# Transposed tiles of x read from DRAM, and two tiles centred after their transpose, in the first layer of a graph network

## What is computed

```python
h = relu(layernorm(x))
# layer 0 (relational convolution)
n = ln_weight * (h * rsqrt(mean(h*h) + 1e-6))
y = n @ W_root + bias + sum over r of segment_mean(n[src] @ W_rel[r], dst)   # r = 0, 1; width 286
x = x + h + elu(y) @ wo_weight
# layer 1 (attention)
g = relu(layernorm(x));  p = g @ W_gat
e = exp(-leaky_relu(p@a_l [src] + p@a_r [dst]))
x = x + g + elu(segment_sum(e * p[dst], src) / (segment_sum(e, src) + 1e-5))
```

## Time and profile before

| | us |
|---|---|
| median of 3 runs | 515.64 |
| the runs | 514.94 to 517.17 |
| the profiled execution, its own time | 514.97 |
| its span | 513.2 |
| PE busy | 495.4 (97%) |
| DVE busy | 374.9 (73%) |
| ACT busy | 226.7 (44%) |
| POOL busy | 74.7 (15%) |

### The profile page before, as it was taken

The page is one execution under the profiler, slowest core; times in us unless marked ns, Lnnn a source line. Parts: engine busy times, 40 slices in busy tenths (PEclk is TensorE's granted clock), DMA queues, the critical chain, the costliest instruction groups (busy, mean ns, idle before and its releaser), DMA issues.

```text
span 513.2 us, 7812 instructions
## 1 busy us (share of the span) xinstructions
PE 495.4 (97%) x2983; PEld 426.2 (83%) x2983; DVE 374.9 (73%) x644; ACT 226.7 (44%) x382; POOL 74.7 (15%) x72
## 2 busy tenths in 40 slices
PE   3999999999999999999999999999999999999996
PEld 2889989988989988898788888888887888888886
DVE  4846885598889999997865555556598878777633
ACT  5865443415966666667632222224233333223211
POOL 1362213100000000000000000000083333322400
PEclk9999999999999999999999999999999999999999
DMA  9872273404013235247911111100022222222211
GB/s 259 228 239 81 80 228 117 127 1 114 2 47 112 84 99 143 81 123 277 319 53 40 41 41 41 41 0 0 1 80 82 83 90 69 81 80 81 70 53 44
DMA packets 22186, 49.15 MB, mean 96 GB/s; under 512 B 4798, under 2 KB 10709, under 8 KB 22018
## 3 DMA queue, kind: packets, MB, share of 16 engines
q1 hardware_dynamic: 20879, 44.66, 29.2%
q10 hardware_dynamic: 1008, 3.67, 2.0%
q0 software_dynamic: 256, 0.26, 0.2%
HBM read 33.05 MB, written 16.85 MB: 97 GB/s over the span
## 4 chain that ended last, share of the span: by engine, by line
PE 86%; DVE 7%; DMA 4%; ACT 2%; issue 1%; SPq 0%; ACTq 0%; DVEq 0%
PE ps L1328 11%; PE ps L1593 9%; PE ps L1595 9%; PE ps L1594 9%; PE ps L1487 8%; PE ps L1574 7%; PE ps L1575 7%; PE ps L1576 7%; PE ps L1397 4%; PE ps L1416 2%; DMA x_scratch<-xt 1%; PE ps L1546 1%; DMA xt<-xh_scratch 1%; PE ps L1560 1%; PE ps L1548 1%; PE ps L1547 1%
## 5 line engine op out<-in xcount | busy, mean ns | idle before, releaser
L1593 PE MATMUL ps<-h_hi,att_hi 125*125 125x512 f32 (+1 forms) x190 | 73.5, 387 | 0.0
L1594 PE MATMUL ps<-h_lo,att_hi 125*125 125x512 f32 (+1 forms) x190 | 72.6, 382 | 0.0
L1595 PE MATMUL ps<-h_hi,att_lo 125*125 125x512 f32 (+1 forms) x190 | 72.5, 382 | 0.0
L1574 PE MATMUL ps<-wg,gT_hi 128*125 128x512 f32 x160 | 63.8, 399 | 0.3 <-DVE wg L1097 0.3
L1575 PE MATMUL ps<-wg,gT_hi 128*125 128x512 f32 x160 | 63.1, 394 | 0.0
L1576 PE MATMUL ps<-wg,gT_lo 128*125 128x512 f32 x160 | 63.0, 394 | 0.0
L1487 PE MATMUL ps<-msg_hi,adj_hi 125*125 125x288 f32 x180 | 50.3, 303 | 0.2 <-ACT adj_hi L596 0.2
L1487 PE MATMUL ps<-msg_lo,adj_hi 125*125 125x286 f32 x180 | 45.9, 295 | 0.0
L471 POOL TENSOR_TENSOR some<-first_att 125x625 f32<-125x625 f32 x1 | 2.4, 2440 | 277.8 <-DVE first_att L1157 277.8
L691 ACT ACTIVATE em<-ps,rinv 125x512 f32<-125x512 f32 (+1 forms) x21 | 14.0, 669 | 64.2 <-DVE hp L1201 64.2
L1595 PEld LDWEIGHTS ps<-h_hi,att_lo 125*125 125x125 f32 x190 | 35.2, 186 | 7.9
(11 more groups left out here) (215 smaller groups left out, 1116.6 us busy)
## 6 DMA issues: line engine op xcount, KB each, us to landing
xt<-in_x SPq DMA_DIRECT2D x10, 448.0 KB
xh_scratch<-xt SPq DMA_DIRECT2D x10, 448.0 KB
xt<-xh_scratch SPq DMA_DIRECT2D x10, 448.0 KB
x_scratch<-xt SPq DMA_DIRECT2D x10, 448.0 KB
x1t<-x_scratch SPq DMA_DIRECT2D x10, 448.0 KB
xr<-x_scratch SPq DMA_DIRECT2D x10, 448.0 KB
out_x<-xr SPq DMA_DIRECT2D x19, 224.0 KB
wg_raw<-in_L_gnn_W ACTq DMA_DIRECT2D x7, 512.0 KB, 7.4
```

What stands on the lines that cost most here:

```text
L1574: M.matmul(to, hi, wg[k][:, 0, cut], start=n == 0, stop=False)
L1593: M.matmul(to, hi[:, s, :], h_hi[:, s, cut], start=s == 0, stop=False)
L1594: M.matmul(to, hi[:, s, :], h_lo[:, s, cut], start=False, stop=False)
L1595: return M.matmul(to, lo[:, s, :], h_hi[:, s, cut], start=False, stop=s == TILES - 1)
```

## The change

- The host hands the kernel a second copy of x, `x_turned`, in which each tile is already transposed (128 partitions, 8 parts of 125 columns). For tiles 4 to 9 SP loads it into `x_t` (`load_x_turned`), a DMA of 500 KB per tile.
- For these tiles PE transposes nothing. It spreads the tile's mean over the partitions of a PSUM bank with one matmul (`means`). DVE subtracts it (`centred`), ACT takes the relu into `hT_hi` (`high_parts`), DVE makes `hT_lo` from `x_t` and `hT_hi` (`turned_low_parts`). The layer norm's scale, which is positive, is left out there and multiplied into the second scale by a small operation in `mean_square`.
- Tiles 0 and 1 are treated alike, but PE transposes the raw x as it comes (`raw_transposed`), ACT copies the mean out of PSUM (`spread`), and DVE's `raw_centred` subtracts it in halves. Their `deviation` and `norm`, which now serve only the residual and the second scale, stand behind the split of most of the weights.
- Tiles 2 and 3 stay as they were.
- `picked` and `windows_transposed` move on PE into the middle of the products of tiles 6 and 8, and `total` into `last_products`. On DVE, `first_rows` is cut in another place.
- At the seam, ACT's `load_wg(6)` and `load_wg(7)` stand behind parts of `turned`, and both engines split weight part 4 one call earlier.

```diff
+            def load_x_turned(t, b):
+                sp.wait_ge(S["hT_lo_rdy"], data(t - 2 if t >= TURNED + 2 else b))
+                sp.dma_start(x_t[b][:], x_turned[t].rearrange("p (k n) -> p k n", n=T)).then_inc(S["xt_in"][b], 16)
...
             for t in range(AHEAD, TILES):
                 store_xh(t, t % 2)
                 if t + 2 < TILES:
                     load_x(t + 2, t % 2)
+                if TURNED + 2 <= t + 1 < TILES:
+                    load_x_turned(t + 1, (t + 1) % 2)
...
+            def high_parts(t, b):
+                act.wait_ge(S["centred"], t - TURNED + 1)
+                act.wait_ge(S["g_ps"], room(t))
+                A.activation(hT_hi[b][:], x_t[b][:], ACT.Relu).then_inc(S["hT_hi_rdy"], 1)
...
+            def raw_centred(t, h):
+                dve.wait_ge(S["hT_ps"], data(t))
+                dve.wait_ge(S["spread"], t + 1)
+                V.tensor_tensor(x_t[t][:, 4 * h:4 * h + 4, :], first_tp(t, h), mean_b[t][:].unsqueeze(1).broadcast_to([P, 4, T]),
+                                ALU.subtract).then_inc(S["raw_centred"], 1)
+            def first_low_parts(t, h, came_in, many, signal):
+                dve.wait_ge(S[came_in], many)
+                V.scalar_tensor_tensor(hT_lo[t][:, 4 * h:4 * h + 4, :], x_t[t][:, 4 * h:4 * h + 4, :], 0.0,
+                                       hT_hi[t][:, 4 * h:4 * h + 4, :].bitcast(F32), ALU.max, ALU.subtract).then_inc(S[signal], 1)
             def mean_square(t):
                 dve.wait_ge(S["rm_rdy"], data(t))
-                V.reciprocal(stats1[:, bass.ds(t, 1), 5], stats1[:, bass.ds(t, 1), 5]).then_inc(S["rms_rdy"], 1)
+                last = V.reciprocal(stats1[:, bass.ds(t, 1), 5], stats1[:, bass.ds(t, 1), 5])
+                if not 2 <= t < TURNED:
+                    last.then_inc(S["rs1_rdy"], 1)
+                    dve.wait_ge(S["rs1_rdy"], t + 1 if t < 2 else t - TURNED + 3)
+                    last = V.tensor_tensor(stats1[:, bass.ds(t, 1), 5], stats1[:, bass.ds(t, 1), 5], stats1[:, bass.ds(t, 1), 2], ALU.mult)
+                last.then_inc(S["rms_rdy"], 1)
+            def centred(t, b):
+                dve.wait_ge(S["xt_in"][b], (t - b) * 8 + 16 - 8 * TURNED)
+                dve.wait_ge(S["mean_ps"], t - TURNED + 3)
+                V.tensor_tensor(x_t[b][:], x_t[b][:], bank(b, P, T).unsqueeze(1).broadcast_to([P, KT, T]), ALU.subtract).then_inc(S["centred"], 1)
+            def turned_low_parts(t, b):
+                dve.wait_ge(S["hT_hi_rdy"], data(t))
+                V.scalar_tensor_tensor(hT_lo[b][:], x_t[b][:], 0.0, hT_hi[b][:].bitcast(F32), ALU.max, ALU.subtract).then_inc(S["hT_lo_rdy"], 1)
+            def step1(t):
+                centred(t, t % 2)
+                messages(t - 2, t % 2, t // 2 - 1)
+                turned_low_parts(t, t % 2)
+                mean_square(t)
+                if t + 1 < TILES:
+                    moments(t + 1, 1 - t % 2, (t + 1) // 2)
...
             def stage1(first, end):
-                pipeline((transposed, 1), (products, 2), steps=(first, end))
+                for t in range(first, end):
+                    products(t, t % 2, t // 2)
+                    if t + 2 < TILES:
+                        means(t + 2)
```

More of the change, by code:

```diff
@@ L49, in rgcn_gat_kernel @@
     AHEAD = 4
+    TURNED = 4
     BAND = 112
@@ L151, in rgcn_gat_kernel @@
         zero_adj_of.close()
+        turned_of = ExitStack()
+        sb(turned_of, "below_x_t", [P, XT_AT // 2], BF16)
+        x_t = [sb(turned_of, f"x_t{b}", [P, KT, T], F32) for b in range(2)]
+        turned_of.close()
         counts = sb(ctx, "counts", [T, TILES, N], U16)
@@ L226, in rgcn_gat_kernel @@
             ("some", [T, TILES // 2, T], F32))
+        mean_b = [over("junk", 32 + 512 * b, f"mean_b{b}", [P, T]) for b in range(2)]
         w_raw, wo_raw = over("w_lo", 0, "w_raw", [P, KT, 2, FB]), over("wo_lo", 0, "wo_raw", [FT, 2, D])
@@ L569, in _ @@
             pads()
-            pipeline((transposed, 1), (messages, 2), (normed, -1), steps=(AHEAD, TILES + 1))
+            transposed(3, 1, 1)
+            for t in range(AHEAD, TILES):
+                messages(t - 2, t % 2, t // 2 - 1)
+                high_parts(t, t % 2)
+                if t + 1 < TILES:
+                    normed(t + 1, 1 - t % 2, (t + 1) // 2)
+            messages(TILES - 2, 0, TILES // 2 - 1)
             for g in range(NG):
@@ L1361, in products @@
                 for n in range(2):
+                    if n == 1 and t == 6:
+                        picked()
+                    if n == 1 and t == TILES - 2:
+                        windows_transposed()
                     last = split_products(bank(2 + 2 * b + n, T, FB), [
@@ L1419, in last_products @@
                 pe.wait_ge(S["zero_used"], NG)
-            first_transposed()
-            products_of(0, 0)
-            transposed(1, 1, 0)
-            products_of(0, 1)
-            for k in range(0, 2):
-                products_of(1, k)
-            for k in range(2, 7):
+            for t in range(2):
+                raw_transposed(t)
+                raw_means(t)
+            for t in range(2):
+                for k in range(0, 3):
+                    products_of(t, k)
+            for k in range(3, 7):
                 products_of(0, k)
@@ L1432, in _ @@
             products_of(1, 7)
-            stage1(AHEAD, 8)
-            picked()
-            stage1(8, 10)
-            windows_transposed()
-            stage1(10, 11)
-            total()
+            transposed(3, 1, 1)
+            stage1(2, TILES - 1)
             last_products()
```

143 lines of the change are left out of this document (90 added, 53 removed).

## The result

| kernel | median of 6 runs | lowest to highest | profiled execution | its span | granted clock |
|---|---|---|---|---|---|
| before | 516.04 us | 514.94 to 517.17 | 514.97 us | 513.2 us | 0.998 |
| changed | 525.30 us | 523.26 to 526.12 | 523.56 us | 521.7 us | 0.990 |

The change makes the kernel slower: 1.0164 times as long, 95% interval 1.0143 to 1.0185, that is 8.5 us with 7.4 to 9.5 (the two medians of the table are 9.3 apart). I had forecast 518.4 and a range up to 521.0. The direction was right, the size was not. The two profiled executions are 8.6 apart (8.5 in span), so they are a fair pair to look for the time in.

The account below looks back on a forecast made before the run. PE, busy 97% of the span, was taken to bound the kernel, with its waits. 514.97 + 5.7 (start) - 4.1 (stage 1) + 3.0 (tail) - 1.2 (seam) = 518.4 us; range 513.3 to 521.0.

Parts of the forecast that it names:

- The start: Up to PE's products of tile 2: late norm of tile 2 and DVE held by POOL's residuals, +5.7 us.
- toss-up: Whether residual(0) catches deviation(1)'s two-input operation, 0.04 us behind its earliest start: +5.0 if not, +6.4 if caught; middle taken.
- Stage 1: From tile 2's products to the last tile's: transposes of six tiles removed, mean matmuls added, fewer low-part waits, -4.1 us.
- 0.3 for tile 9's statistics: Within stage 1's sum: PE waits 0.3 us for the statistics of tile 9.
- loads of transposed tiles come late: Rival: tile 8's x_t load stands behind a store queued behind window-span DMAs; 1 to 2 us more on DVE, 520.5; chance 0.15.
- The tail: End of stage 1: PE's window groups wait for DVE's keys and first rows, +2.7, plus total moved there, +0.3.
- The seam: PE's 1.03 wait behind ACT's loads of weight parts 6 and 7 goes: -1.2 us, at worst 0.
- would take it back: At the seam: PE's 0.29 wait for a weight part would cancel the gain, had DVE not moved part 4 ahead.
- One-column operations aren't held: Rival at the start: residuals don't hold one-column DVE operations; tile 2's products at 38.1, sum 516.2; chance 0.17.
- No DVE operation of the start meets a residual: Rival at the start: no holds there, tile 2's products at 36.3, sum 513.5; chance 0.18.
- the signs I had named for being right: Tile 2's product near 40, norm(2) past 32, L946 and L948 over 1 us, 9.7 product spacing, window-group idling, no 1.03 seam wait.
- The signs I had named for being wrong: Products of tile 2 before 37, PE waiting for a low part between tiles 4 and 8, window groups without a wait.

Follow-up runs that it names:

- no_meetings: Changed kernel, with POOL starting its residuals of tiles 0 to 2 each only after the next tile's deviation is made: 1.0066 of before, 520.17 us.
- six_tiles: Changed kernel without its start: tiles 0 and 1 normed and then transposed as in the kernel before: 1.0007 of before, 516.93 us.
- kept_busy: Changed kernel with matmuls nobody reads put into four of PE's waits, the waits themselves kept: 1.0092 of before, 521.59 us.
- pauses: Kernel before, with PE made to wait twice for nothing it needs, behind the products of tiles 3 and 5: 1.0133 of before, 523.36 us.
- early_loads: Changed kernel, each transposed tile's load put ahead of the store of the tile before on SP's queue: 1.0157 of before, 524.90 us.
- loads_residual: early_loads, with POOL starting the residual of tile 8 only behind DVE's low part of tile 8: 1.0123 of before, 522.56 us.
- early_norms: Changed kernel, deviations and norms of tiles 0 and 1 moved ahead of weight part 4 on ACT, part 3 on DVE: 1.0091 of before, 521.29 us.
- six_best: six_tail, with the statistics of tile 9 made ahead of the messages of tile 6 on DVE: 1.0055 of before, 519.56 us.
- all_mended: Changed kernel with early norms, residuals 0 and 1 right behind them, 2 and 3 behind tile 3's deviation, and six_tail's stage 1 end: 1.0020 of before, 517.68 us.
- six_tail: six_tiles with early loads, residual(8) behind low part 8, windows transposed before tile 8's products, keys before tile 7's messages: 0.9979 of before, 514.69 us.

## Why the prediction was right and wrong

**The start, +5.7 forecast, +6.7 measured: the mechanism held.** norm(2) was late because DVE and ACT made the first norms behind weight parts, and DVE was held by POOL. no_meetings, which takes only the holds away, moved the first product by 4.1. The toss-up fell on its upper side: the one-column operation came 0.02 behind the residual's start and was caught. The middle that I took was a value the kernel could not have; of a coin with sides at 5.0 and 6.4 one side has to be named. That is 0.7 of the 1.0. The other 0.3 fit the statistics of tile 1, for which I let DVE go from one tile to the next, while x of tile 1 came 1.04 us later.

**Stage 1, -4.1 forecast, -1.1 measured: the step that failed.** The removed and added work was as priced: without the wait for the mean (2.13) and the half clock behind it (1.70) the stretch gives -4.9, against the -4.4 of my terms without the 0.3 for tile 9's statistics. That 0.3 was 2.13. I had the mechanism as the last rival, "loads of transposed tiles come late", at 0.15, but gave it 1 to 2 us "on DVE, which has them to spare until the keys". I followed DVE's queue forward to the keys and left out that the statistics of tile 9 stand in it, with PE waiting for them long before. On the cause of the late load I was half right. On SP's queue it stood behind another load, which I had not seen, and that one waited for the store of tile 7 to land. But the store did take 7.3 with the spans' copy under way, against 3.1 and 4.0 for the two before it; in the kernel before and in six_tiles the store behind the spans took 7.3 and 7.4 too. That the spans slowed it is argued from this, not tried. The rival had nearly the right event, at 2.1 in its sum, where wait and clock together cost 3.5.

**No term for the clock.** PE's waits were priced at their own length. In the sum a wait of 2 to 3 us can cost 1.7 more. kept_busy shows it in this kernel and pauses in the one before, though in kept_busy's profile 1.0 of the 1.75 won came back as a longer wait for the first window group: this term and the tail's lean on each other. The changed kernel's profiled execution came 5.2 above my sum; one such stretch on PE's path is 1.7 of it, the wait ahead of that stretch 1.8 (2.13 less the 0.3). The profiled execution has the highest granted clock of the changed kernel's six, 0.990 against a median of 0.9865. That is 1.8 us of full clock more in the median, an estimate, and the median time is 1.7 above the profile. So it probably holds one stretch more. Run by run the two don't go together strictly (525.05 us at 0.990, 523.26 at 0.987), so this isn't shown.

**The tail, +3.0 forecast, +1.2 measured.** The first window group waited 0.80, not 2.7. The rows were ready at 114.8, 2.6 later than forecast, but PE wanted them at 114.1, 4.6 later. six_tiles shows the wait at 1.74 with PE on time. A term that depends on another's size can't be summed as if it stood alone.

**The seam, -1.2 forecast, +0.2 measured.** -0.7 up to the second half, then +0.9, of which 0.62 is more waiting for weight parts. My forecast named a weight part as what "would take it back", and it did, but not by the order of the parts. Ahead of the last of them DVE adds a tile of `xh`, and waited 2.30 for its load where it had waited 1.41 before. The difference is the 0.9. In kept_busy, with the same code at the seam, it waited 0.83, and PE for no weight part at all. Both rows, changed and kept_busy:

```profile
257.84 1.22 DVE L1158 TENSOR_TENSOR xt<-ps,xt 125x1024 f32<-125x1024 f32 x1 [2.30 <-DMA xt<-xh_scratch]
```

```profile
255.64 1.23 DVE L1158 TENSOR_TENSOR xt<-ps,xt 125x1024 f32<-125x1024 f32 x1 [0.83 <-DMA xt<-xh_scratch]
```

Over all 14 profiles PE's wait for weight parts grows with this wait of DVE's: none at 0.50 to 1.26, 0.29 at 1.41, 0.47 at 1.58, up to 1.0 at 2.42. Why the load lands late in some executions stays open.

**Not forecast at all:** 0.45 in stage 2 (0.77 instead of 0.41 for `yT_hi`, 0.37 instead of 0.23 for `adj_hi`), and 1.05 for the landing of the last store, which no instruction of the change touches. SP's last wait for it is 1.6 in before, 2.7 in the changed kernel and 1.9 to 3.1 in the others, 3.1 in pauses, which ends with the code of before. So it looks like the spread of this landing, with the profile of before at its lower end.

**The rivals.** "One-column operations aren't held" is refuted by 2.38, 1.61 and 2.40 us. "No DVE operation of the start meets a residual" didn't happen by itself; no_meetings made it so and gained its 4 to 5. Of the signs I had named for being right, the 2 to 3 us of idling at the first window group didn't come (0.80). The signs I had named for being wrong didn't come either, yet the number was wrong: none of them would have shown the wait for the mean or the clock.

## What to carry to other kernels

In these traces a residual on POOL held the DVE operations with two SBUF inputs that it met, of whatever size, until its end, and `tensor_scalar` operations with one SBUF tensor (2.51 instead of 0.35, 2.31 instead of 0.42) as well. So look in the order of DVE's queue for the ones of both kinds, the small ones too, that stand between POOL's start and something PE wants, and start POOL behind them; and expect that when one delay is removed the engine arrives inside the next. When a PE-bound kernel gets a new wait of some 2 us, reckon with a half-clock stretch behind it (1.7 us here, and it came behind some such waits and not behind others), or fill the wait with matmuls nobody reads, few enough to end before what PE waits for.

## What the runs showed of the hardware that I had not expected

**The idle stretch alone doesn't tell whether the clock falls.** In these profiles half clock followed waits of 1.78 (no_meetings, at 111.15), 1.90 (early_loads, at 41.44), 2.06 (no_meetings, at 37.10), 2.06 (loads_residual, at 41.26), 2.13, 2.77 and 3.81, and did not follow 1.36, 1.62, 1.78 (early_norms, at 110.67), 2.06 (the changed kernel, at 41.24) or 2.19 (early_norms, at 97.99). Waits of one length come out both ways; the changed kernel and loads_residual have even the same code there. So a kernel with such waits can have executions 1.7 us apart. It also came behind short gaps close together: at 111 in six_best, behind 0.95 and 0.74, and at 11 to 12 in early_norms, all_mended and kept_busy, behind 0.75 and 0.30, soon after PE had begun.

**PE's first matmuls run at about half rate with the granted clock shown as 1.00.** In six_tiles a pair of products of 860 columns together takes 1.08 and 0.88 at 10.5 to 11.4 and 0.56 from 12.08 on; in six_tail, whose start has the same code, pairs still take 0.92 at 12.58 and 0.89 at 14.83. The transposes of tile 1 take 1.87 there and 1.02 in six_tiles. The first product of tile 2 came 1.65 later; most of it is this, 0.40 a wait for `hT_hi` that six_tiles doesn't have. The Trainium skill, page TensorE: Matmul & The Clock Gate, section "What's actually happening", has the clock at its lower level by default, before the engine has been busy; the durations agree, the granted clock of the profile's windows does not show it there.

**A gather on POOL beside a DVE operation with two SBUF inputs didn't hold it.** In loads_residual the low part took 1.19 while POOL's indirect DMA instruction ran from 96.07 to 97.28.
